# Layer 2 attention: row sums by TensorE and a logarithm, in place of normalised probabilities

## The reference

```python
q, k, v = h @ Wq, h @ Wk, h @ Wv          # 16 heads of 64
q, k = apply_rope(q), apply_rope(k)
scores = q @ k.T / 8, causal mask
attn = softmax(scores, axis=-1)
out = (attn @ v) @ Wo + bo
x = x + gate * out
```

## Time and profile before

| | |
|---|---|
| median of 3 runs | 1713.69 us (1708.1 to 1717.39) |
| profiled execution, its own time | 1712.15 us |
| its span, first to last instruction | 1710.3 us |
| mean granted TensorE clock | 0.892 of 2.4 GHz |
| busy over the span | PE 1280.4 us (75%), PEld 734.0 (43%), DVE 1093.0 (64%), ACT 829.1 (48%), POOL 623.6 (36%) |
| attention stage of layer 2 | about 384 to 782 us |

### The profile page before, as it was taken

One profiled execution on the slowest core, in us unless ns is written; L12 is line 12 of the kernel. 1 busy time (PEld: TensorE's weight loads), 2 busy tenths in 40 slices (PEclk: granted clock), 3 DMA queues, 4 the chain that ended last, 5 costly groups with the idle time before them and its releaser, 6 DMA issues.

```text
span 1710.3 us, 27876 instructions
## 1 busy us (share of the span) xinstructions
PE 1280.4 (75%) x10366; PEld 734.0 (43%) x10366; DVE 1093.0 (64%) x2509; ACT 829.1 (48%) x2019; POOL 623.6 (36%) x577
## 2 busy tenths in 40 slices
PE   8754009548999999996878888767777687777768
PEld 6222009514555555552345555434444433444433
DVE  4366503227999999994257777646776644677653
ACT  4651003124566665664666666545555434555542
POOL 1110160345565565652012222145555404555520
PEclk8966559757999999998999999869999997999989
DMA  7000115560000000002000000000000000000000
GB/s 252 1 0 0 48 40 202 125 69 1 1 1 1 1 1 1 1 1 87 0 1 2 2 2 2 1 27 1 2 2 2 2 1 1 2 2 2 1 2 25
DMA packets 15265, 38.95 MB, mean 23 GB/s; under 512 B 3572, under 2 KB 8054, under 8 KB 14496
## 3 DMA queue, kind: packets, MB, share of 16 engines
q1 hardware_dynamic: 13088, 34.70, 5.7%
q0 software_dynamic: 2048, 2.54, 2.1%
HBM read 33.07 MB, written 5.77 MB: 23 GB/s over the span
## 4 chain that ended last, share of the span: by engine, by line
PE 37%; DVE 31%; ACT 15%; issue 10%; POOL 4%; DMA 1%; SPq 0%; DVEq 0%; POOLq 0%; ACTq 0%
DVE soft L1145 6%; DVE bank L1134 5%; PE bank L1694 4%; PE bank L1377 4%; ACT win_soft_alibi L1384 3%; PE bank L1359 3%; ACT win_soft_local L1384 3%; PE bank L1916 3%; DVE rope_part L1125 3%; PE bank L1349 2%; PE bank L195 2%; ACT win_softT_alibi L1392 2%; PE bank L1702 2%; PE bank L1713 2%; PE bank L203 2%
## 5 line engine op out<-in xcount | busy, mean ns | idle before, releaser
L1079 ACT ACTIVATE soft<-bank,neg_max 128x512 f32<-128x512 f32 (+3 forms) x256 | 133.2, 535 | 123.9 <-DVE neg_max L1134 122.7
L1863 POOL TENSOR_TENSOR win_part<-win_part,scaled_tab 128x512 f32<-128x512 f32 x64 | 81.2, 1269 | 200.7 <-DVE win_part L1805 200.7
L1145 DVE TENSOR_SCALAR soft<-soft,exp_inv 128x128 f32<-128x128 f32 (+1 forms) x192 | 137.5, 768 | 2.2
L1694 PE MATMUL bank<-shifted,att_w 128*128 128x512 f32 x128 | 78.9, 748 | 78.2 <-DVE v_even L1832 69.1
L1201 POOL TENSOR_TENSOR rope_part<-rope_part,rope_tab 128x512 f32<-128x512 f32 x64 | 82.2, 1285 | 145.9 <-DVE rope_part L1125 145.8
L1419 POOL TENSOR_TENSOR win_soft_alibi<-win_soft_alibi,win_inv_alibi 128x384 f32<-128x384 f32 x64 | 52.9, 827 | 218.3 <-DVE win_inv_alibi L1403 218.3
L1134 DVE CUSTOM_DVE_ANT_0 bank<-bank,att_mask 128x512 f32<-128x512 f32 (+3 forms) x256 | 118.5, 512 | 6.9 <-PE bank L1007 6.9
L1091 ACT ACTIVATE softT<-bank 128x512 f32<-128x512 f32 x160 | 93.6, 612 | 26.5 <-PE bank L1021 26.5
L1021 PE MATMUL bank<-ident,soft 128*128 128x128 f32 x640 | 99.7, 279 | 1.9 <-ACT softT L1091 1.9
L1007 PE MATMUL bank<-k_rope,q_rope 64*128 64x128 f32 (+3 forms) x512 | 97.6, 479 | 2.2 <-POOL k_rope L1206 2.2
L1384 ACT ACTIVATE win_soft_local<-bank,win_neg_max_local,rq 128x128 f32<-128x128 f32 x256 | 96.2, 463 | 5.7 <-DVE win_neg_max_local L1815 5.7
(11 more groups left out here) (329 smaller groups left out, 3331.0 us busy)
## 6 DMA issues: line engine op xcount, KB each, us to landing
moe_w<-in_moe_w SPq DMA_DIRECT2D x8, 960.0 KB, 6.1
y_tok<-in_moe_w SPq DMA_DIRECT2D x8, 960.0 KB, 5.6
att_w<-in_att_w SPq DMA_DIRECT2D x1, 1536.0 KB, 8.3
att_w<-in_local_w SPq DMA_DIRECT2D x1, 1536.0 KB, 8.9
xg_dram<-zeros SPq DMA_DIRECT2D x5, 256.0 KB, 9.2
y_dram<-y_slot SPq DMA_DIRECT2D x16, 80.0 KB
wmod<-in_wmod SPq DMA_DIRECT2D x1, 1152.0 KB, 7.6
x<-in_x SPq DMA_DIRECT2D x4, 256.0 KB, 4.6
```

The lines of the kernel that those rows point to most:

```text
L1079: nc.scalar.activation(soft[par][:, hd, TILE_AT[t]:TILE_AT[t] + keys(t)], score_bank(u, s, hd)[:, at:at + keys(t)], ACT.Exp, scale=-1.0, b ...
L1145: last = nc.vector.tensor_scalar(p, p, exp_inv[:, par, n:n + 1], None, ALU.mult)
L1694: last = pe.matmul(bank[5 * piece][:, :], w, tokens(b, 0, T), start=True, stop=True)
L1863: nc.gpsimd.tensor_tensor(swapped, swapped, scaled_tab[:, 2 * j + 1, :], ALU.mult) \
```

## The change

The probabilities are no longer normalised, neither by VectorE nor by GpSimd, and the exponentials lose their accumulator output. Instead TensorE makes a second pass over `softT` behind the value products (`att_sums`): the same four chunks for both heads, but with 64 columns of the constant matrix `mean` (every element 1/128) as the stationary operand, into bank 6. Each partition of a head then holds that head's row sum over 128, for every query. ScalarE takes the logarithm of it (scaled by 128), then the exponential of minus that (`inverse`), and VectorE multiplies bank 7 by the result where it had copied it (`heads`).

Around that, the order changes. Bank 6 now holds transposes T1 and T3 and the sums, and T1 waits until the logarithm has been read out of it (`sum_logged`). The output projection moves from behind q to behind T1, `heads` on VectorE from the front of the iteration to behind the first rotary piece, and `add` behind the second group of maxima. `inverse` stands on ScalarE between the copies of T0 and T1.

```diff
@@ att_transpose, att_sums @@
-            if f < 2:
-                pe.wait_ge(sem("p_normed"), 2 * u + f + 1)
-            if f == 1:
-                pe.wait_ge(sem("p_normed_pool"), u + 1)
-            if 5 * u + f >= 2:
-                pe.wait_ge(sem("pt_ready"), 5 * u + f - 1)
+            if f == 0:
+                pe.wait_ge(sem("s_exp"), 8 * u + 8)
+            if f == 1 and u:
+                pe.wait_ge(sem("sum_logged"), u)
+            elif 5 * u + f >= 2:
+                pe.wait_ge(sem("pt_ready"), 5 * u + max(f - 1, 0))
...
+        def att_sums(pe, u):
+            for jc in (0, 1, 3, 2):
+                for hd in range(2):
+                    lo, at = 64 * hd, CHUNK_AT[hd, jc, jc]
+                    last = pe.matmul(bank[6][lo:lo + 64, 128 * jc:T], mean[:, lo:lo + 64], softT[:, at:at + T - 128 * jc],
+                                     start=(jc == 0), stop=(jc == 2))
+            last.then_inc(sem("sum_raw"), 1)
@@ att_pe @@
-                if out:
-                    att_output(pe, u - 1)
                 if work:
                     att_transpose(pe, u, 0)
                 if score:
                     att_scores(pe, u + 1, 1)
                 if work:
                     att_transpose(pe, u, 1)
+                if out:
+                    att_output(pe, u - 1)
...
                     att_values(pe, u)
+                    att_sums(pe, u)
@@ att_exps, att_act @@
-                                         bias=neg_max[:, par, n:n + 1], accum_out=exp_sum[:, par, n:n + 1]) \
-                      .then_inc(sem("s_exp"), 1)
+                                         bias=neg_max[:, par, n:n + 1]).then_inc(sem("s_exp"), 1)
...
+            def inverse(u):
+                act.wait_ge(sem("sum_raw"), u + 1)
+                nc.scalar.activation(sum_log[:, :], bank[6][:, :], ACT.Ln, scale=float(C)).then_inc(sem("sum_logged"), 1)
+                act.wait_ge(sem("sum_logged"), u + 1)
+                if u:
+                    act.wait_ge(sem("pv_read"), u)
+                nc.scalar.activation(sum_inv[:, :], sum_log[:, :], ACT.Exp, scale=-1.0).then_inc(sem("sum_inv"), 1)
...
                 if work:
                     transposed(u, 0)
+                if out:
+                    inverse(u - 1)
+                if work:
                     transposed(u, 1)
@@ att_dve @@
-            def norm(u):
...
-                if u >= 2:
-                    dve.wait_ge(sem("p_normed_pool"), u - 1)
-                for half in range(2):
-                    dve.wait_ge(sem("s_exp"), 8 * u + STEP_END[1 + half])
...
-                tiles(0, (0, 1)).then_inc(sem("p_normed"), 1)
-                tiles(1, (0, 1)).then_inc(sem("p_normed"), 1)
...
-                nc.vector.tensor_copy(head_out[u % 2][:, :], bank[7][:, :]).then_inc(sem("pv_read"), 1)
+                dve.wait_ge(sem("sum_inv"), u + 1)
+                nc.vector.tensor_tensor(head_out[u % 2][:, :], bank[7][:, :], sum_inv[:, :], ALU.mult) \
+                  .then_inc(sem("pv_read"), 1)
...
-                if out:
-                    heads(u - 1)
                 if score:
                     att_maxes(dve, u + 1, 0)
                 if project:
                     att_rope(dve, u + 2, 0)
                 if out:
-                    add(u - 1)
+                    heads(u - 1)
                 if score:
                     att_maxes(dve, u + 1, 1)
+                if out:
+                    add(u - 1)
```

More of the change, by code:

```diff
@@ L965, in adaln_blocks @@
         neg_max = tmp_sb("neg_max", [128, 2, 8])
-        exp_sum = tmp_sb("exp_sum", [128, 2, 8])
-        exp_inv = tmp_sb("exp_inv", [128, 2, 8])
+        sum_log = tmp_sb("sum_log", [128, T])
+        sum_inv = tmp_sb("sum_inv", [128, T])
         head_out = [tmp_sb(f"head_out{i}", [128, T]) for i in range(2)]
@@ L1012, in att_transpose @@
         def att_transpose(pe, u, f):
-            if f < 2:
-                pe.wait_ge(sem("p_normed"), 2 * u + f + 1)
-            if f == 1:
-                pe.wait_ge(sem("p_normed_pool"), u + 1)
-            if 5 * u + f >= 2:
-                pe.wait_ge(sem("pt_ready"), 5 * u + f - 1)
+            if f == 0:
[4 more added lines that the diff above has]
+                pe.wait_ge(sem("pt_ready"), 5 * u + max(f - 1, 0))
             for i, (hd, jc, t) in enumerate(FILLS[f]):
                 at = TILE_AT[t] + 128 * jc
-                last = pe.transpose(bank[5 + (5 * u + f) % 2][:, 128 * i:128 * i + 128],
-                                    soft[u % 2][:, hd, at:at + 128], ident[:, :])
+                last = pe.transpose(bank[5 + f % 2][:, 128 * i:128 * i + 128], soft[u % 2][:, hd, at:at + 128], ident[:, :])
             last.then_inc(sem("pt_raw"), 1)
+        def att_sums(pe, u):
[5 more added lines that the diff above has]
+            last.then_inc(sem("sum_raw"), 1)
         def att_values(pe, u):
@@ L1090, in transposed @@
                 act.wait_ge(sem("pt_raw"), 5 * u + f + 1)
-                nc.scalar.activation(softT[:, 512 * f:512 * f + 512], bank[5 + (5 * u + f) % 2][:, :], ACT.Copy) \
+                nc.scalar.activation(softT[:, 512 * f:512 * f + 512], bank[5 + f % 2][:, :], ACT.Copy) \
                   .then_inc(sem("pt_ready"), 1)
@@ L1099, in values @@
                                      ACT.Copy).then_inc(sem("proj_read"), 1)
+            def inverse(u):
[5 more added lines that the diff above has]
+                nc.scalar.activation(sum_inv[:, :], sum_log[:, :], ACT.Exp, scale=-1.0).then_inc(sem("sum_inv"), 1)
             for u in range(-2, UNITS + 1):
-                score, project, work = 0 <= u + 1 < UNITS, u + 2 < UNITS, 0 <= u < UNITS
+                score, project, work, out = 0 <= u + 1 < UNITS, u + 2 < UNITS, 0 <= u < UNITS, u >= 1
                 if score:
@@ L1194, in att_dve @@
                     att_maxes(dve, u + 1, 2)
-                    norm(u + 1)
         def att_pool(pool):
@@ L1209, in att_pool @@
             pool.wait_ge(sem("att_tables"), 32)
[L1210 to L1216, removed]
             for u in range(UNITS):
@@ L1220, in att_pool @@
                 rope(u, 1)
-                if u >= 1:
-                    norm(u - 1)
-            norm(UNITS - 1)
         next_block()
```

## The result

The changed kernel takes 1821.2 us in the median (1820.25 to 1822.15, 4 runs) against 1715.54 for the one before (4 runs): 1.0624 times as long, 95% interval 1.0589 to 1.0659. That is 106 us more; 1827 was predicted, 115 more. The profiled execution has a span of 1819.0 us.

What follows compares the result with a forecast made beforehand. VectorE was taken to set the pace at 11.77 us per unit, TensorE close behind. TensorE's 11.31 + 2.30 sums + 0.96 and 0.90 waits make 15.47; 31 x 3.70 = 114.7 us on 1712.15 gives 1827, range 1790 to 1852.

Steps and rivals of the forecast that it cites:

- TensorE's own need: Attention stage before the change: TensorE needs 11.31 us per unit without waits, 4% behind VectorE's 11.77.
- the rival at 1570 us: Attention stage: TensorE has room for the sums, VectorE stays the bound at 7.19 us per unit; chance 0.03.
- The sums: TensorE's second pass behind the value products: 2.30 us per unit, bounds 2.2 to 2.4.
- The wait at T1: TensorE at T1 waits for ScalarE's logarithm: start at 4.48 instead of 3.52 us, 0.96 us per unit.
- The wait at O: TensorE at the output projection waits for VectorE's head product: start at 5.87 us, 0.90 us per unit.
- if either went alone: Attention stage: either wait alone removed gives about 1798 us; one or both waits gone has chance 0.12.
- From a unit to the kernel: Attention stage: 31 full distances of 3.70 us more, 114.7 us; first unit's missing waits and last unit's tail about cancel.
- No wait at v or V: TensorE at the value projection and value products: inputs just in time, priced at nothing, bound 0.3 us at v.
- the rival of a falling clock: TensorE's waiting lowers its clock in a tenth of the attention stage: 43 us more, 1870 us; chance 0.06.
- Sums only: Attention stage: both waits absorbed, 1.84 us more per unit, 1769 us; one or both waits gone has chance 0.12.

Runs made afterwards that it cites:

- no_normalising: The kernel before without the normalising products on VectorE and GpSimd, and without sums: 1695.12 us against 1712.72, ratio 0.9892.
- sums_unused: The kernel before with the pass of sums added behind the value products, results not used, normalising kept: 1766.37 us against 1712.72, ratio 1.0314.
- inverse_first: The changed kernel with the logarithm and its exponential at the front of ScalarE's iteration: 1772.38 us, ratio 1.0342 to the kernel before.
- add_late: heads_early with VectorE's add moved behind the second rotary piece: 1759.64 us against 1711.32 for the kernel before, ratio 1.0292.
- one_chunk: The changed kernel with only the first of the four chunks of sums: 1777.88 us, ratio 1.0366 to the kernel before.
- heads_early: inverse_first with VectorE's head product also ahead of the first rotary piece: 1775.53 us on one chip (ratio 1.0395), 1779.36 on another.
- act_normalises: The kernel before with GpSimd's two normalising tiles given to ScalarE, no sums: 1694.88 us against 1707.95, ratio 0.9919.

## Why the prediction was right

- **TensorE's own need.** I read it from the starts as 11.31 us per unit, with VectorE's 11.77 4% above it. With the normalising taken out, the unit is 11.32. The sum was right, but its parts were not: I put q at 0.86 and O at 0.96, and without a wait it is q 0.96 and O 0.86 (`no_normalising`, 582.06 to 583.88). O takes 0.96 only behind a wait. This step carried the forecast: the weight-load share of half, by which there was ample room, would have led to the rival at 1570 us. The rival is refuted by `sums_unused` (53.7 us) and `no_normalising` (17.6 us).
- **The sums.** 2.30 predicted from the value products, 2.26 measured. What they add to TensorE's need is less, 13.47 - 11.32 = 2.15 in `sums_unused`, because the value products in front of them are 0.10 shorter.
- **The wait at T1.** 0.96 predicted, 0.71 measured, and that is the term that was mis-sized. The logarithm took 0.60 us where the layer norm's took 0.69; it starts 0.48 behind the copy of T0, not 0.55; and T1's place without a wait is 3.62 us into the iteration, not 3.52, since q in front of T0 takes 0.96 without a wait. T1 starts at 4.33, where 4.48 was laid out.
- **The wait at O.** O was laid out at 5.87 and starts at 5.82. Since T1 is earlier the wait is longer, 1.00 for 0.90. With the bare need of 13.52 for 13.61, the unit is 15.23 us instead of 15.47. Of the 3.46 more than before, the sums less the old waits are 1.75 and the new waits 1.71.
- **The two waits are not two prices.** For the time if either went alone the prediction gives 1798 us, as if each cost its own length. In its own walk O starts at 5.87 whatever T1 does, so without T1's wait O would only wait longer, and nothing would be won; O's start, which the head product sets, carries the whole 1.71 us. No run took T1's wait away alone, so this follows from the order of the queue and is not measured.
- **From a unit to the kernel.** 31 x 3.46 = 107.3 us; the medians are 105.7 apart, the profiled executions 108.7. From the first S0 to the last it is 102.7 (470.4 us against 367.7), since the first two distances grew by only 0.17 and 2.29. Another 3.7 came behind the last S0. So the tail made up for most of the units that lacked the waits, as the prediction said. The last 2.3 lie ahead of the first S0, where both kernels do the same.
- **What gave it back.** `inverse_first` and `add_late` gave back 1.42 and 1.81 us per unit by order alone (the 1.81 has in it the 0.10 that O takes less without a wait); `one_chunk` showed that the two parts add.
- **No wait at v or V.** That held in the changed kernel in most units, but only just, as the prediction said ("just in time"). In one unit of each batch v waited 0.5 us. The prediction had named a wait at v as a sign of being wrong, and had not looked at these four units; since they were 0.59 us longer before as well, it cost nothing. As soon as O came another 0.3 us earlier, in `heads_early`, 0.3 us of waiting appeared at v in every unit. My expectation of that run left this out.
- **The clock.** It stayed at 1.00 (550 to 600 us) with 1.71 us of waiting in 15.23. Nothing speaks for the rival of a falling clock.
- **Sums only.** The two waits were not absorbed. That rival's time, 1769 us, is near what the kernel takes once the queues are reordered (`add_late`, 1759.64).

## What to carry to other kernels

Before work is moved off the engine that sets the pace, read from start to start how far behind it the next engine is. Here it was 0.45 us in 11.77, so relief could bring 4% of the stage and 1% of the kernel, and what was given to that next engine beyond 0.45 us was lost time. In a pipeline of in-order queues the place of an instruction is part of its cost: a logarithm whose input was long ready stood behind two exponentials of the next unit, and putting it in front gave back 1.42 of the 3.46 us lost per unit. Where a wait is removed, look at once for what had been just in time behind it.

## What the runs showed of the hardware

- The logarithm with an immediate scale and bias took 598 ns in the mean, the layer norm's, with a bias from a tile, 687, both from a bank of 512 columns. The Trainium skill, "ScalarE: Activation LUTs", section What ACT_TABLE_LOAD costs, says that each per-partition operand adds about 93 ns. The rows agree with 89, and with that page read the wait at T1 would have been sized 0.09 us better. Both rows are groups over the whole execution of the changed kernel:

```profile
L1110 ACT ACTIVATE sum_log<-bank 128x512 f32<-128x512 f32 x32 | 19.1, 598 | 4.1 <-PE bank L1028 4.1
...
L234 ACT ACTIVATE ln_log<-bank,eps_col 128x512 f32<-128x512 f32 x40 | 27.5, 687 | 17.1 <-PE bank L203 15.9
```

- VectorE's products of 256 columns by a number per partition took 636 ns in the mean beside GpSimd's products and 348 once GpSimd had handed those to ScalarE; those of 384 columns, beside GpSimd's rotary sum in both kernels, 1433 ns in both. First the kernel before, then `act_normalises` (groups by line and shape, 408 us onward):

```profile
L1145 DVE TENSOR_SCALAR soft<-soft,exp_inv 128x384 f32<-128x384 f32 x30 | 43.0, 1433 | 0.0
...
L1145 DVE TENSOR_SCALAR soft<-soft,exp_inv 128x256 f32<-128x256 f32 x60 | 38.1, 636 | 0.0
```

```profile
L1155 DVE TENSOR_SCALAR soft<-soft,exp_inv 128x384 f32<-128x384 f32 x30 | 43.0, 1433 | 0.0
...
L1155 DVE TENSOR_SCALAR soft<-soft,exp_inv 128x256 f32<-128x256 f32 x60 | 20.9, 348 | 0.0
```

  The Trainium skill, "SBUF — State Buffer", section Who interferes with whom, says that VectorE in a two-port mode and GpSimd take a shared pair of ports in turn, each for a whole instruction. These rows agree with that; the ports themselves no run shows.
- A matmul against a constant matrix cost about what one against data did: 2.26 us for the sums in front of S0, 2.30 for the value products in the same place in the kernel before.
- What a piece costs from start to start depended on its neighbours. The value products took 2.30 us in front of S0 and 2.20 to 2.21 in front of the sums. The output projection took 0.96 us behind a wait (611.74 to 612.70) and 0.86 without one (`no_normalising`, 583.02 to 583.88). Why, no run shows.
- An exponential of 512 columns took 0.68 and 0.66 us to the next start with its accumulator output (585.96, 586.64, 587.30 in the kernel before), and two without it took 1.23 together (607.89 to 609.12 in the changed kernel): about 0.05 us less each.
